# A graph-attention and mixture-of-experts kernel: the activation transposes placed between the two halves of the next first-layer product

## The reference

```python
logits = pooled @ router_w.T + router_b            # pooled: mean over the nodes of a graph
top_v, top_i = jax.lax.top_k(logits, TOP_K)        # 2 of 4 experts for each graph
gates_k = jax.nn.softmax(top_v, axis=-1)
h = jnp.einsum('bld,edh->belh', x, w1) + b1[None, :, None, :]     # 384 -> 768
h = jnp.stack([_ACTS[i](h[:, i]) for i in range(e)], axis=1)      # gelu, silu, mish, gelu
out = jnp.einsum('belh,ehd->beld', h, w2) + b2[None, :, None, :]  # 768 -> 384
y = jnp.einsum('be,beld->bld', gate, out) + x
# then a layer norm of y
```

## Time and profile before

| | |
|---|---|
| median of 3 runs | 1630.68 us (1630.11 to 1630.93) |
| the profiled execution's own time | 1629.46 us |
| span of its trace, first to last instruction | 1627.5 us |
| PE busy | 1588.3 us, 98% |
| DVE busy | 1211.8 us, 74% |
| ACT busy | 969.9 us, 60% |
| mean granted clock of TensorE | 0.997 |

### The profile page before, as it was taken

One profiled execution on the slowest core, in us unless ns is written; L12 is line 12 of the kernel. 1 busy time (PEld: TensorE's weight loads), 2 busy tenths in 40 slices (PEclk: granted clock), 3 DMA queues, 4 the chain that ended last, 5 costly groups with the idle time before them and its releaser, 6 DMA issues.

```text
span 1627.5 us, 46196 instructions
## 1 busy us (share of the span) xinstructions
PE 1588.3 (98%) x12720; PEld 1524.6 (94%) x12721; DVE 1211.8 (74%) x3752; ACT 969.9 (60%) x2882; POOL 684.5 (42%) x1105
## 2 busy tenths in 40 slices
PE   8999999999999999979999999999999999999998
PEld 7999999999999999869999999999999999999997
DVE  5788788887888878766866666776777867677776
ACT  6899999998888988852433333443444434343442
POOL 3778888777877777631111111111111111111112
PEclk9999999999999999999999999999999999999999
DMA  6433333344444433672111111111211112111111
GB/s 187 157 116 124 114 111 120 120 159 160 150 157 154 161 118 114 225 309 84 47 58 57 58 60 60 59 60 60 61 60 45 56 59 60 60 60 60 60 45 45
DMA packets 93517, 163.94 MB, mean 101 GB/s; under 512 B 10304, under 2 KB 73792, under 8 KB 92096
## 3 DMA queue, kind: packets, MB, share of 16 engines
q1 hardware_dynamic: 91664, 145.01, 27.3%
q10 hardware_dynamic: 1584, 15.73, 2.6%
HBM read 96.22 MB, written 64.49 MB: 99 GB/s over the span
## 4 chain that ended last, share of the span: by engine, by line
PE 90%; DVE 4%; ACT 2%; issue 2%; DMA 1%; DVEq 1%; POOL 1%; ACTq 0%; POOLq 0%; SPq 0%
PE bank L488 69%; PE bank L562 5%; PE bank L697 5%; PE bank L515 3%; PE bank L585 3%; PE bank L602 2%; PE bank L571 1%; PE bank L594 1%; DVE inverse L1430 1%; ACT prob L769 1%; DVE half_t L1423 1%; DVE inverse L1426 1%; DMA xu_scratch<-xu 1%; ACT at_hi L991 0%; DVEq L1307 0%
## 5 line engine op out<-in xcount | busy, mean ns | idle before, releaser
L488 PE MATMUL bank<-w_hi,ut_in 128*128 x1536 | 421.4, 341 | 0.4
L488 PE MATMUL bank<-w_both,at_hi 128*128 x1524 | 389.8, 336 | 9.2 <-DVE at_lo L1395 9.2
L769 ACT ACTIVATE prob<-att,heads 128x128 f32<-128x128 f32 x768 | 297.9, 400 | 13.6 <-DVE heads L1159 11.7
L488 PEld LDWEIGHTS bank<-w_both,at_hi 128*128 128x128 f32 x1524 | 275.3, 188 | 14.2 <-issue 14.1
L488 PEld LDWEIGHTS bank<-w_hi,ut_in 128*128 128x128 f32 x1536 | 279.6, 188 | 1.4 <-issue 1.4
L488 PE MATMUL bank<-w_lo,ut_in 128*128 x768 | 256.9, 335 | 0.0
L488 PE MATMUL bank<-w_both,at_lo 128*128 x762 | 255.7, 336 | 0.0
L991 ACT ACTIVATE at_hi<-bank,gate_col 128x384 fp32r<-128x384 f32 x254 | 133.8, 578 | 200.0 <-PE bank L697 198.0
L913 ACT ACTIVATE hid<-hid 128x384 f32<-128x384 f32 x192 | 95.1, 527 | 254.7 <-DVE hid L1316 252.6
L1316 DVE TENSOR_TENSOR hid<-bank,b_wide 128x384 f32<-128x384 f32 x256 | 130.8, 552 | 117.9 <-PE bank L488 111.6
L1395 DVE SCALAR_TENSOR_TENSOR at_lo<-bank,gate_col,at_hi 128x384 fp32r<-128x384 f32 x254 | 144.9, 612 | 96.1 <-ACT at_hi L991 96.0
(11 more groups left out here) (140 smaller groups left out, 3506.9 us busy)
## 6 DMA issues: line engine op xcount, KB each, us to landing
xu_scratch<-xu SPq DMA_DIRECT2D x64, 384.0 KB, 2.3
xz<-xu_scratch SPq DMA_DIRECT2D x64, 384.0 KB, 3.2
x_in<-in_x SPq DMA_DIRECT2D x32, 384.0 KB, 3.4
xu<-in_x SPq DMA_DIRECT2D x32, 384.0 KB, 4.3
ut_scratch<-ut_out SPq DMA_DIRECT2D x64, 192.0 KB, 1.9
ut_in<-ut_scratch SPq DMA_DIRECT2D x64, 192.0 KB, 2.4
out_dram<-xz SPq DMA_DIRECT2D x64, 192.0 KB, 1.9
w_lo<-in_L_ffn_w SPq DMA_DIRECT2D x4, 1152.0 KB, 6.1
```

The costliest lines, as they stand in the source:

```text
L488: last = nc.tensor.matmul(acc, lhs[c][a], rhs[c][b], start=start and n == 0, stop=stop and n == len(terms) - 1)
L769: nc.scalar.activation(prob[g][:, hh, :], att[g][:, head, :], ACT.Exp, bias=neg_max[g][:, head:head + 1], scale=-1.0, accum_out=row_sum[g] ...
```

## The change

Four things are changed.

- On PE, step (b, k) now issues the first half of the first layer of job i, then the transposes of job i-2, then the second half of the first layer, then the second layer of job i-2.
- PE, SP and POOL no longer have the loop: `every_expert_step` writes all 66 steps out and waits for `routed` to reach 2 ahead of graph 4. DVE and ACT keep `expert_steps`.
- DVE's routing of the second half of the graphs stands at the end of its step and is spread over one more step: `route_rest` at (2, 0), the second choice at (2, 1), factors and gates at (3, 0). ACT's `tanh_of_gap(1)` moves from (2, 1) to (3, 0), and SP's load of `xz[3]`, with its wait for `routed`, from graph 2 to the front of graph 3's step.
- On DVE, the output biases stand ahead of `finish`; those of graph 0 are added at (1, 1) as before, those of graph 1 at (2, 0) and no longer at (2, 1).

```diff
@@ -291,6 +291,13 @@
...
                     step(i * (B // 2 - 4) + 4 + j, j % 4, i * (B // 8 - 1) + 1 + j // 4)
             for b in range(B - 4, B + 2):
+                step(b, b % 4, b // 4)
+
+        def every_expert_step(engine, step):
+
+            for b in range(B + 2):
+                if b == 4:
+                    engine.wait_ge(routed, 2)
                 step(b, b % 4, b // 4)
 
...
@@ -459,6 +466,10 @@
...
 
             def expert_step(b, m, lap):
+                if isinstance(b, int) and b == 3:
+
+                    sp.wait_ge(routed, 2)
+                    load_xz(3, 3)
                 finish(b, m)
                 if isinstance(b, int) and b == 0:
...
@@ -466,16 +477,12 @@
...
                     sp.dma_start(b2_wide[:].rearrange("p e d -> p (e d)"), b2.rearrange("(o e) d -> o (e d)", o=1).partition_broadcast(P)).then_inc(b2_loaded, 16)
                     load_rest()
-                if isinstance(b, int) and b == 2:
-
-                    sp.wait_ge(routed, 2)
-                    load_xz(3, 3)
                 if graph(b, -2):
                     send(b - 2, (m - 2) % 4)
...
                     refill(b + 1, (m + 1) % 4, lap + (m + 1) // 4)
 
-            expert_steps(sp, lambda b, m, lap: expert_step(b, m, lap) if graph(b, 0) else send(b - 2, (m - 2) % 4))
+            every_expert_step(sp, lambda b, m, lap: expert_step(b, m, lap) if graph(b, 0) else send(b - 2, (m - 2) % 4))
             for m in range(4):
                 sp.wait_ge(out_stored[m], 16 * (B // 4))
...
@@ -618,10 +625,10 @@
...
                 return pe.value_load(cell, min_val=0, max_val=E - 1)
 
-            def first_layer(b, k, m, lap, e):
+            def first_layer(b, k, m, lap, e, halves=range(2)):
                 i = b * K + k
                 reached(pe, ut_split, b + 1)
-                for s in range(2):
+                for s in halves:
                     reached(pe, hid_done, 2 * i + s - 3)
                     if isinstance(i, int) and i == 1:
...
@@ -629,7 +636,8 @@
...
                                          [tuple(w[:].rearrange("p e c f -> p (e c f)")[:, bass.ds(e * (DC * F) + (c * F + s * HALF), HALF)]
                                                 for w in (w1_hi, w1_lo)) for c in range(DC)])
-                last.then_inc(h_mm, 1)
+                if 1 in halves:
+                    last.then_inc(h_mm, 1)
 
             pe.wait_ge(ident_ready, 2)
...
@@ -720,12 +728,15 @@
...
                     if graph(b, -1):
                         second_e = choice(b - 1, k)
+                        if graph(b, 0) and not ahead:
+
+                            first_layer(b, k, m, lap, first_e, range(1))
                         if not last_job(b - 1, k):
                             transpose_act(b - 1, k)
...
                             transpose_act(b - 1, k + 1)
                     if graph(b, 0) and not ahead:
-                        first_layer(b, k, m, lap, first_e)
+                        first_layer(b, k, m, lap, first_e, range(1, 2))
                     if isinstance(b, int) and (b, k) == (1, 0):
                         transpose_u(B - 1)
...
@@ -735,7 +746,7 @@
...
                         logits(1)
 
-            expert_steps(pe, expert_step)
+            every_expert_step(pe, expert_step)
 
         @block.scalar
...
@@ -1004,8 +1015,6 @@
...
             def expert_step(b, m, lap):
                 for k in range(K):
-                    if isinstance(b, int) and (b, k) == (2, 1):
-                        tanh_of_gap(1)
                     if graph(b, 0):
                         e = choice(b, k)
...
@@ -1016,6 +1025,8 @@
...
                     if isinstance(b, int) and (b, k) == (0, 1):
                         take_u(B - 1)
+                    if isinstance(b, int) and (b, k) == (3, 0):
+                        tanh_of_gap(1)
                     if graph(b, 0):
                         invert(b, k, e)
...
@@ -1134,7 +1145,7 @@
...
                     nc.gpsimd.tensor_tensor(x1, x1, lnb_wide[:], ALU.add).then_inc(x_based, 1)
 
-            expert_steps(pool, expert_step)
+            every_expert_step(pool, expert_step)
 
         @block.vector
...
@@ -1467,39 +1478,39 @@
...
                 if (b, k) == (1, 1):
                     route_expert(1, 0)
+                if (b, k) == (2, 0):
                     route_rest()
-                if (b, k) == (2, 0):
+                if (b, k) == (2, 1):
                     route_greatest(1, 1)
                     route_expert(1, 1)
-                if (b, k) == (2, 1):
+                if (b, k) == (3, 0):
                     route_factors()
                     route_gates(1)
 
             def expert_step(b, m, lap):
+                experts = []
                 for k in range(K):
                     if graph(b, 0):
-                        e = choice(b, k)
+                        experts.append(choice(b, k))
                         if not isinstance(b, int) or b > 0:
-                            take_hidden(b, k, m, lap, e)
+                            take_hidden(b, k, m, lap, experts[k])
 
                     if k == 0 and graph(b, -2):
                         add_experts(b - 2, (m - 2) % 4)
-                    if k == 1 and graph(b, -2):
-                        finish(b - 2, (m - 2) % 4)
-                    if isinstance(b, int):
-                        route_second_half(b, k)
-                    if k == 1:
-
-                        if isinstance(b, int) and b == 1:
+
+                    if isinstance(b, int) and (b, k) in ((1, 1), (2, 0)):
+                        if b == 1:
                             dve.wait_ge(b2_loaded, 16)
                         for late in range(K):
-                            if isinstance(b, int) and b in (1, 2):
-                                add_output_bias(b - 1, late, b - 1, 0, choice(b - 1, late))
+                            add_output_bias(b - 1, late, b - 1, 0, choice(b - 1, late))
+                    if k == 1:
                         for late in range(K):
                             if graph(b, 0) and (not isinstance(b, int) or b > 1):
-                                add_output_bias(b, late, m, lap, choice(b, late))
+                                add_output_bias(b, late, m, lap, experts[late])
+                        if graph(b, -2):
+                            finish(b - 2, (m - 2) % 4)
                     if graph(b, 0):
-                        activate_first(b, k, e)
+                        activate_first(b, k, experts[k])
                     if k == 0 and graph(b, -1):
                         split_act_lo(b - 1, 1, m - 1)
...
@@ -1508,9 +1519,11 @@
...
                         weigh(1)
                     if graph(b, 0):
-                        activate_second(b, k, e)
+                        activate_second(b, k, experts[k])
                     if k == 0 and graph(b, 1) and not (isinstance(b, int) and b < 1):
                         rest_of_ut(b + 1, (m + 1) % 4, lap + (m + 1) // 4)
+                    if isinstance(b, int):
+                        route_second_half(b, k)
 
             expert_steps(dve, expert_step)
...
```

## The result

The changed kernel takes **1670.57 us** (1667.69 to 1672.66), the kernel before 1630.62 us beside it: a ratio of 1.0242, 95% interval 1.0228 to 1.0256. It is 40 us slower. The forecast was 1663.6 us with a range of 1646 to 1679. The profiled execution took 1671.75 us; it is the one compared here with the 1629.46 us of before.

A forecast was written before the change was run, and what follows sets the result against it. PE's work plus its gaps was taken as the bound. New gaps of 46.8 us, less 15.6 old and 1.6 at the start, add 29.6; the clock adds 3.4: 1662.5 us profiled, 1663.6 us median, range 1646 to 1679.

The forecast's parts named there:

- Undisturbed jobs: Second layer due before its split is ready in jobs without Mish delays: 0.13 us lost each, 14.0 us for 108.
- the restart: Extra time until PE's second layer is under way after a late split's first half ends: 0.27 us, taken from job 43.
- the load of weights is in time: Rival: a layer released just at its due time loses nothing, undisturbed jobs cost 0, total 1648 us; chance 0.14.
- Odd Mish jobs: Seven odd Mish jobs standing alone: their second layer waits for a late split, 1.60 us lost each, 11.2 us.
- Even Mish jobs: Three even Mish jobs standing alone: the next graph's first layer waits for `ut_split`, 2.09 us lost each, 6.3 us.
- Pairs: Three pairs of neighbouring Mish jobs: a second layer loses 2.58 us, the next first layer 2.09; 14.0 us together.
- The loop: PE's jump back goes, but DVE's jump stays and delays job 63's split: 1.3 us come back.
- The start: First expert steps: the stall at 757.22 goes, graph 3's rows load late; 1.6 us gained, within 1 either way.
- The clock: Half-clock stretches on PE behind new idle stretches: two taken, 3.4 us; bounds 0 to 17 us.

The follow-up runs named there:

- e3: The changed kernel with the even jobs' wait for `z_added` taken ahead of the first layer, so their second layer waits for `at_lo` alone: 1666.39 us.
- e6: The changed kernel with Mish left out, its expert's hidden values going through gelu: 1636.94 us.
- e11: The changed kernel with the transposes back ahead of the whole first layer and the output biases reading the expert's number again from memory: 1623.96 us.
- e8: The kernel before with only the steps of PE, SP and POOL written out: 1628.60 us.

## Why the prediction held, and where its terms were off

The sign, the mechanism and the size held; the median lay 7 us above the forecast. Some 2 us of this nearness are luck: the forecast for the profiled execution was 1662.5 us and it took 1671.75, 9.3 more, but the median stands 1.2 us below that execution now and stood 1.2 us above it before. The ledger runs from T to T: from job 7 to job 126 the changed kernel takes 1655.22 - (777.96 - 1.56) = 878.8 us, 57.7 over 821.1, where the prediction had 46.8, and 3.4 more for the clock. (The 1.56 us are the half product that now stands ahead of the transposes.)

- **Undisturbed jobs.** Forecast 0.13 us each, 14.0 for 108 (the even Mish jobs and the second job of each pair among them); measured 0.15 behind odd and 0.24 behind even jobs, 0.20 on average, 20.3 us for the 102 without those. This is the largest miss, and a term that was mis-sized: job 43, from which I took the restart, is an odd job with one wait in front of its layer, and half of the jobs have two (e3). The trace of before held a hint that the prediction doesn't use: the layer at 757.22, of an even job, is released by the first half of this split, which ends at 756.96, 0.26 us ahead of it and not 0.16:

```profile
756.35 1.14 DVE L1395 SCALAR_TENSOR_TENSOR at_lo<-bank,gate_col,at_hi 128x384 fp32r<-128x384 f32 x2
```

- **The rival "the load of weights is in time"** is refuted: the loss is there in every job, in e6 too, without Mish. The Trainium skill, "TensorE: Matmul & The Clock Gate", section "Step-by-step: what each phase is for", says that loads of weights are pulled ahead of matmuls in flight. The trace agrees as long as the split is early: in the kernel before the load stands 0.17 us ahead of its matmul. It doesn't help a load that waits for the split itself, which here starts with its matmul (1205.39).
- **Odd Mish jobs.** Forecast 1.60 us each, 11.2; the seven intervals are 1.47 to 1.87 us over 6.90, 12.2 us together. Five of them are higher by the 0.35 us that e11 traces to the register.
- **Even Mish jobs.** Forecast 2.09 and 0.13, that is 2.22 over 6.90; the three intervals are 9.12, exactly that.
- **Pairs.** Forecast 14.0; the intervals behind jobs 9 and 10, 75 and 76, 101 and 102 are 6.17, 4.78 and 6.14 us over twice 6.90, 17.1 together, half-clock stretches included. The middle pair is what the prediction had without a stretch (4.67 and the 0.13 of its second job), the other two lie 1.4 us higher. So the stretch at 1280 cost almost nothing: it slowed the second layer ahead of graph 39's first layer, which had to wait for DVE anyway, and that wait shrank to 0.23 us from the 1.8 of the other pairs.
- **The loop.** PE's jump is gone and job 63 has lost 1.47 us, forecast 1.3. e8 shows that without the new place of the transposes, too, half of the jump comes back.
- **The start.** Forecast 1.6 us gained, measured 0.5 lost (776.40 against 775.88). The changed kernel is 0.7 us behind already ahead of the expert stage, where the two programs are the same. The late load of graph 3's rows cost less than forecast: jobs 5 and 6 together take 1.4 us over twice 6.90. The gain was lost at job 0, whose second layer starts at 727.19 and not at 724.83, behind a half-clock stretch at 710 that the profiled execution of before doesn't have; a second one follows at 727. That the change makes this loss is not shown: e8, whose instructions up to there are those of before, has stretches at 709 and 726 too and starts that layer at 725.47.
- **The clock.** I gave 3.4 us for two stretches. The profiled execution has five that before had not, and one of before is gone; three of them are in the pairs. Which idle stretches are followed by one I could not foretell, and the runs don't tell it either.

Where the gain of the idea went is plain in the waits: the half product did cover the wait for activated values (2.6 us in three waits). The time was taken from the other side of the transposes, where the chain of ACT and DVE had no more than 1.7 us to give and 1.56 plus the restart of 0.27 were asked.

## What to carry to other kernels

Moving an instruction within a full queue doesn't only give its inputs more time; it takes the same time from whoever needs its output. Measure that chain end to end first (here transposes to split, 2.08 us, plus 0.27 for the restart), compare it with the work that is left between, and multiply what is missing by the number of jobs: 0.2 us in every one of some hundred jobs cost 20 us, beside 27 us in all the waits that PE's view lists. The waits of the loads (PEld) list both.

## What the runs showed that I had not expected

A matmul whose weights come only just in time starts 0.16 us behind the releasing DVE instruction and loses 0.10 us more in its first pair; with a second, long reached wait in front of it the start is at 0.27 us. The view of waits of the matmuls lists neither, that of the loads lists 123 such places, 56.9 us, against the 57.7 us of the ledger. Half-clock stretches of 3.4 us began in all three pairs of Mish jobs behind idle stretches of 1.8 to 2.2 us, and one of them was nearly free, because a later wait had a fixed end.
